# The end of the gates in a four-model chain: where attention 5 opens, and where ScalarE's table is loaded

## What is computed

```
x_norm = rms(x) ; z = x_norm @ Wz + bz ; k = x_norm @ Wk + bk
gamma  = clip(sigmoid(gelu(z @ Wg1 + bg1) @ Wg2 + bg2) * sigmoid(gelu(k @ Wgc1 + bgc1) @ Wgc2 + bgc2), 1e-6, 1 - 1e-6)
def step(h, (z_t, g_t)):                         # 100 steps, one after the other
    gate = sigmoid(z_t @ Wgz + bgz + h @ Wgh + bgh)
    return (1 - gate) * h + gate * z_t + g_t * h
q = (x_norm @ Wq + bq) @ Awq + abq               # 8 heads
mem_out = softmax(q . (ctx @ Awk + abk) / sqrt(32)) . (ctx @ Awv + abv) @ Awo + abo
x = x + h_seq + mem_out + 0.1 * (x_norm @ Wv + bv) ; x = x + ffn(rms(x))
```

## Time and profile before

| | us |
|---|---|
| median of 3 runs | 1533.06 (1532.91 to 1533.58) |
| the profiled execution | 1533.99 |
| its span, first to last instruction | 1532.3 |
| TensorE busy | 1459.3 (95%) |
| VectorE busy | 759.5 (50%) |
| ScalarE busy | 651.7 (43%) |
| GpSimd busy | 261.4 (17%) |
| mean granted TensorE clock | 0.991 |

### The profile page before, as it was taken

One profiled execution on the slowest core, in us unless ns is written; L12 is line 12 of the kernel. 1 busy time (PEld: TensorE's weight loads), 2 busy tenths in 40 slices (PEclk: granted clock), 3 DMA queues, 4 the chain that ended last, 5 costly groups with the idle time before them and its releaser, 6 DMA issues.

```text
span 1532.3 us, 28708 instructions
## 1 busy us (share of the span) xinstructions
PE 1459.3 (95%) x12202; PEld 939.0 (61%) x12202; DVE 759.5 (50%) x1591; ACT 651.7 (43%) x1394; POOL 261.4 (17%) x443
## 2 busy tenths in 40 slices
PE   9999899999899999999999999999899999989998
PEld 8665556565555566555677765554566667655576
DVE  1576767777633365211233332323777777852132
ACT  2665555656643432111334432224555454443244
POOL 1443200101000010000112210000245544500000
PEclk9999999999999999999999999999999999999999
DMA  4321000000000100000200000000000000020032
GB/s 164 106 61 40 11 29 2 2 2 1 2 28 1 62 22 1 21 0 0 83 1 1 1 1 28 0 1 7 28 2 2 2 2 2 2 81 0 0 99 62
DMA packets 19562, 36.85 MB, mean 24 GB/s; under 512 B 2058, under 2 KB 17386, under 8 KB 18282
## 3 DMA queue, kind: packets, MB, share of 16 engines
q1 hardware_dynamic: 19434, 35.01, 6.9%
HBM read 33.36 MB, written 1.64 MB: 23 GB/s over the span
## 4 chain that ended last, share of the span: by engine, by line
PE 87%; DVE 6%; ACT 5%; issue 1%; DVEq 0%; ACTq 0%
PE psum L447 40%; PE psum L863 11%; PE psum L497 8%; PE psum L593 6%; PE psum L633 6%; DVE maxima L1571 3%; PE psum L589 3%; ACT probs L1210 3%; PE psum L532 2%; PE psum L968 2%; PE psum L996 1%; PE psum L977 1%; PE psum L1009 1%; PE psum L549 1%; PE psum L563 1%
## 5 line engine op out<-in xcount | busy, mean ns | idle before, releaser
L1571 DVE TENSOR_REDUCE maxima<-psum 100x2 f32<-100x722 f32 (+3 forms) x332 | 245.9, 760 | 144.4 <-PE psum L532 119.1
L447 PE MATMUL psum<-x_resid,weights 128*128 128x400 f32 x832 | 295.8, 506 | 3.0 <-ACT probs L1210 1.7
L447 PEld LDWEIGHTS psum<-x_resid,weights 128*128 128x128 f32 x832 | 157.4, 192 | 119.6 <-issue 5.8
L1210 ACT ACTIVATE probs<-psum 128x800 f32<-128x800 f32 (+3 forms) x224 | 168.0, 787 | 100.0 <-PE psum L593 99.8
L863 PE MATMUL psum<-weights 128*128 128x400 f32 x512 | 174.8, 499 | 0.7 <-DVE maxima L1571 0.7
L447 PE MATMUL psum<-weights,ctx_t 128*128 128x256 f32 (+1 forms) x576 | 157.4, 397 | 3.1 <-ACT ctx_t L1132 2.4
L863 PEld LDWEIGHTS psum<-weights 128*128 128x128 f32 x512 | 97.2, 190 | 75.1 <-DVE maxima L1571 0.8
L497 PE MATMUL psum<-ctx_t,weights 128*128 128x361 f32 x384 | 135.3, 478 | 1.6 <-DVE weights L1846 0.8
L447 PEld LDWEIGHTS psum<-weights,ctx_t 128*128 128x128 f32 (+1 forms) x576 | 99.8, 186 | 44.1 <-issue 10.7
L1132 ACT ACTIVATE weights<-psum 128x400 f32<-128x400 f32 (+2 forms) x80 | 37.9, 475 | 205.5 <-PE psum L447 205.4
L633 PE MATMUL psum<-probs,values 128*32 128x100 f32 (+5 forms) x3328 | 113.4, 255 | 0.9 <-DVE q_then_o L1629 0.3
(11 more groups left out here) (168 smaller groups left out, 2076.0 us busy)
## 6 DMA issues: line engine op xcount, KB each, us to landing
weights<-in_w SPq DMA_DIRECT2D x2, 3072.0 KB, 9.6
staged<-in_ctx SPq DMA_DIRECT2D x32, 128.0 KB, 2.2
values<-in_ctx SPq DMA_DIRECT2D x32, 128.0 KB, 2.2
weights<-in_w SPq DMA_DIRECT2D x3, 1024.0 KB, 4.8
weights<-in_src SPq DMA_DIRECT2D x1, 2368.0 KB, 14.0
weights<-in_w SPq DMA_DIRECT2D x1, 2048.0 KB, 7.9
weights<-in_tw SPq DMA_DIRECT2D x2, 1024.0 KB, 5.1
staged<-in_ctx SPq DMA_DIRECT2D x16, 105.0 KB, 2.2
```

Source lines behind the costliest of these rows:

```text
L447: i = nc.tensor.matmul(PS[0:rows, bk, 0:n], lhs, rhs, start=k == 0, stop=k == len(terms) - 1)
L1210: nc.scalar.activation(PT[0:kn, k % PROBS_KEPT, :, 0:n], PS[0:kn, bk:bk + 2, 0:n], ACT.Exp).then_inc(act_results, mark("act", f"{t} p{b} { ...
L1571: nc.vector.reduce_max(top, src, AX).then_inc(dve_results, mark("dve", f"{t} m{b} {j}"))
```

## The change

```
-OPEN_AT = ((0, 0, 0, 0), (0, 1, 2, 4), (0, 1, 4, 1))
+OPEN_AT = ((0, 0, 0, 0), (0, 1, 2, 0), (0, 1, 0, 9))
...
                 advance(opening, OPEN_AT[2][g])
             for _ in opening:
                 pass
+            nc.scalar.preload_act_table_set("exp_and_others")
             if due(f"gm{NG - 1}"):
                 act.wait_ge(dve_results, at(f"gm{NG - 1}"))
```

## The result

| | before | changed |
|---|---|---|
| median of 8 runs | 1533.19 us (1529.89 to 1534.82) | 1530.07 us (1526.37 to 1532.08) |
| the profiled execution | 1533.99 | 1528.34 |
| its span | 1532.3 | 1526.6 |

The ratio is 0.9977, with a 95% interval of 0.9968 to 0.9986. The time fell by 3.12 us where 1.86 had been forecast. It lies in the range, but no change lies outside the interval, and by the medians the gain is just over the 0.2% (3.07 us) on which only 0.05 had been put.

The account below looks back on a forecast made before the run. TensorE, busy 95% of the span, bounds the kernel, so only its idles before the scan can be won: 1533.06 - 1.86 = 1531.2 us, with step 1 earlier and the rest following; range 1529.7 to 1533.3.

Parts of the forecast that it names:

- Steps 1 to 5: End of gates, from gz2 to the scan's step 1: reordered TensorE, VectorE and table load bring step 1 1.86 us earlier.
- The drain behind a table load: Behind the moved load: forecast took none; a skill-page drain of some 1380 ns would cut the gain to 1.4 us.
- Step 6: SyncE's 1 MB load of f1 starts some 9 us earlier, beside VectorE's work; claimed cost: nothing.
- Rival (a): Maxima behind split3: the new wait is dearer, 0.1 us at each of ten steps, time 1532.2; chance 0.13.
- (d): Behind the scan's start: another pace turns the 1.86 us into waits, no gain, time 1533.1; chance 0.10.
- (b): Thinned stretch at the gates' end: clock falls behind the idles, time 1533.2 or 1534.7; chance 0.07.
- so the whole rest moves with it: Everything behind step 1 of the scan keeps its order and comes 1.86 us earlier, TensorE nearly always at work.
- (c): Behind the scan: the shift changes the fall at 1357; without it 1529.6 us, at twice the length 1532.8; chance 0.10.
- the fall at 1357: Behind attention 5's 2.41 us idle: TensorE's granted clock drops to 0.50, put at 1.6 us as a whole.
- faster by over 0.2%: Whole kernel: a gain of over 3.07 us, near only with (c) on top of the forecast; chance 0.05.

Follow-up runs that it names:

- order_only: Kernel before with only the new row of slot numbers, without the early table load; 0.9995 of the kernel before (0.9986 to 1.0004).
- load_only: Kernel before with only the early table load, in the old slots; 1.0002 of the kernel before (0.9992 to 1.0012).
- before_late_again: Second profile of the kernel before with 29 products of ones added ahead of step 1 of the scan; one timed execution took 1531.96 us.
- after: First profile of the changed kernel, with both edits against the kernel before; profiled execution 1528.34 us, span 1526.6.
- keys_first: Changed kernel with k1 moved directly behind group 3's gates and VectorE's last gate multiplication ahead of the maxima; 0.9984 of the kernel before (0.9972 to 0.9995).
- before_filled: Kernel before with 36 products of ones filling TensorE's 2.41 us idle at the end of attention 5; 1.0002 of the kernel before (0.9993 to 1.0011).
- keys_first_filled: keys_first with 36 products of ones filling the 2.41 us idle at the end of attention 5; 0.9981 of the kernel before (0.9972 to 0.9990).
- before_again: Kernel before, nothing edited, one more profile; path 26.67 us, rest 430.48 us, one fall at 1130.
- keys_first_late: keys_first with nine products of ones ahead of step 1 of the scan; 0.9987 of the kernel before (0.9978 to 0.9996).
- after_fourth: Changed kernel, nothing edited, a fourth profile; 1534.21 us in its one timed execution, no fall behind the gates.

## Why the prediction was wrong, point by point

**Steps 1 to 5, the path: right.** Laid beside the forecast, in the old trace's time (2.10 added): gz3 at 1082.14 (forecast 1082.14), gA3 1085.02 (1084.83), v0 0 1086.70 (1086.38), m0 0 1089.21 (1089.11), k1 1091.80 (1091.72), mt0 1094.33 (1094.23), st0 0 1095.69, s1 0 ahead of it without an idle, the load 1095.57 (1095.5), m1 0 1097.23 (1097.22), st0 1 1098.25 (1098.25), Tanh 1098.40 (1098.40), step 1 1099.66 (1099.70). The steps in front are 0.2 to 0.3 late, since gz3's records took 2.88 and not 2.69 and the gates 1.68 and not 1.55; what follows on VectorE came only 0.10 late (m0 0), and the end doesn't see it. The wait ahead of s0 3 was 0.19, not 0.5. Laying the new order over old durations gave 1.86 for a measured 1.90.

**The drain behind a table load.** The load ends at 1095.00 in order_only and Exp starts at 1095.02. Nor is there room for one ahead of the load: in the changed kernel it starts at 1093.47, 0.02 behind the evacuation that ends at 1093.45. In load_only Exp follows the load's end by 0.99 us, held by gm3:

```profile
1097.37 1.28 ACT L1415 ACT_TABLE_LOAD   x1
1099.64 0.84 ACT L1210 ACTIVATE probs<-psum 128x800 f32<-128x800 f32 x1 [0.98 <-DVE weights L1925]
```

The Trainium skill, page "ScalarE: Activation LUTs", section "What ACT_TABLE_LOAD costs", has a drain of some 1380 ns more for each switch. None of these loads shows it or has the room for it, and the measurement decides.

**Step 6, the DMA: right, as far as seen.** SyncE issues the load at 1084.60 in the new trace and at 1095.34 in the old, 8.6 us earlier counted from gz2. In the new one it runs beside the split and the maxima, and these take what they took: 0.99 us, and 3.35 for four (a pitch of 0.81, 0.82 before). The prediction's own ground, that instructions ahead of the one at 1096.77 have the same length, stands on no row of that form in rows 4. No run tests the transfer by itself; the rest of 429.0 us, the same with and without the change (before_late_again against after), leaves nothing for it.

**Rival (a)** didn't come: the new waits cost no more than the sum had for them. They are not free, since keys_first, which takes k1 and gm3 from behind the maxima, has a path 0.66 us shorter. **(d)** didn't come either. **(b)** didn't in the changed kernel, whose stretch kept 1.00, but did in order_only, which has nearly the same idles there. Its mechanism was real, its condition was not the length of the idle.

**The failed step is the sentence "so the whole rest moves with it", with the chance of 0.10 for (c).** The sum took the fall at 1357 as a part of the program that moves with it, and (c) as an independent accident. But the rest is not a block: whether the clock falls behind its idles hangs on where in time these stand, and a shift of 1.9 us, the change's own effect, took them off. The missing term is a fall less, 1.65 us in the traces and 0.9 to 1.15 by the means. That the time of 1530.07 lies in the range is the work of (c), which set the range's lower end, and not of the sum. (c)'s size was well put (1.6, and the time 1529.6), although the group that it started from had lost 1.2 us and not 1.1: it takes 1.51 at full clock, and the 1.61 of rows 2 is another group's. With what the runs showed, its chance should have been the forecast's, or near it, and "faster by over 0.2%" then far above 0.05. What could have been seen beforehand is less than this: the trace of before has the fall, and shows two idles of 1.61 and 1.29 without one; nothing in it tells what a shift will do. But it does tell that the fall is worth about as much as the whole change, and that the shift applies to it. Even odds on it would have been the honest figure.

**What stays open.** Why the clock falls behind an idle at some places and not at others is not explained by any view here; the table only says at which it did. It is not the time since the span's start, since gz2 starts anywhere from 1071.81 to 1078.73 in these profiles and the falls behind don't care. How often the changed kernel has a fall in executions that nobody profiled is open too. In before_filled, whose fall behind the 2.41 us is done away with, a gain in the executions that have their fall there should show; none did, but the interval reaches from 1.1 us less to 1.7 more. And keys_first_filled, with its idle filled and no fall, measured 1530.0 by its mean, where path and rest would give some 1529: the sum of path and falls holds to about 1 us in the timed runs, not better.

## What to carry to other kernels

When a kernel's span is nearly all TensorE, split two profiles at a common instruction ahead of the change and one behind it, and compare the pieces: the path of the change is then exact to 0.1 us, while whole times scatter by 1.5. Look where the granted clock falls, and treat each such fall behind the change as a term that the change may add or take away, even where it is hundreds of microseconds later and its own idle stays as it is. And measure each edit alone, and profile it: here the order alone would have been put down as no gain by its time, and its path shows 1.47 us.

## What the runs showed of the hardware

- The granted clock fell to 0.50 behind an idle of 1.02 us (1130 of before_again) and behind 1.09 and 0.37 (1097 of order_only), and stayed at 1.00 behind 2.41 us in all four profiles of the changed kernel. The length of an idle by itself decided nothing between 1.0 and 2.4 us; where it started, counted from an earlier rise of the clock, told falls from none in all 17 profiles. The Trainium skill, page "TensorE: Matmul & The Clock Gate", section "HAM oscillation — how this bites in real kernels", says that waits between groups of matmuls can bring the lower clock back each time. The traces agree that the falls behind the gates stand behind waits, and show that the same wait may have one or not.
- One fall costs 1.4 to 1.7 us (the rest of 430.4 to 430.7 us against 429.0), 0.1% of this kernel.
- Filling an idle with products of ones removes the fall there and may leave one elsewhere: no gain could be seen in before_filled, and 1.4 us in keys_first_filled against keys_first_late.
- An ACT_TABLE_LOAD took 1.28 us, and 0.02 us lay between it and the ACTIVATE behind it (order_only, 1095.00 to 1095.02).
- Executions of one kernel differ in how often the clock falls ahead of the gates, and their spans by up to 5.9 us with it, with the same program (1526.6 in after, 1532.5 in after_fourth).
